# A mixture of experts on one core: a third shared tile in front of the expert blocks, table groups and gathers at other units

## The reference

```
x = x + self_attention(layernorm(x))            # 16 heads, one shared key/value head, causal
x = x + cross_attention(layernorm(x), ctx, pos) # 32 heads, axial rotary positions
h = layernorm(x)                                # 2048 tokens
probs = softmax(h @ router_w.T)                 # 16 experts
top 4 of 16, weights divided by their sum
routed = sum over the 4: (silu(h @ w_gate[e]) * (h @ w_up[e])) @ w_down[e] * weight     # 176 wide
shared = (silu(h @ sh_gate) * (h @ sh_up)) @ sh_down                                    # 704 wide
x = x + routed + sigmoid(h @ sh_gate_w) * shared
```

## Time and profile before

| what | us |
|---|---|
| median of three runs | 776.66 |
| profiled execution: its own time | 777.8 |
| its span | 776.0 |
| TensorE (PE) busy | 687.4 (89%) |
| VectorE (DVE) busy | 401.1 (52%) |
| POOL busy | 359.9 (46%) |
| ScalarE (ACT) busy | 301.4 (39%) |

### The profile page before, as it was taken

The page is one execution under the profiler, slowest core; times in us unless marked ns, Lnnn a source line. Parts: engine busy times, 40 slices in busy tenths (PEclk is TensorE's granted clock), DMA queues, the critical chain, the costliest instruction groups (busy, mean ns, idle before and its releaser), DMA issues. The chain is left out here.

```text
span 776.0 us, 18811 instructions
## 1 busy us (share of the span) xinstructions
PE 687.4 (89%) x6959; PEld 528.3 (68%) x6959; DVE 401.1 (52%) x917; ACT 301.4 (39%) x676; POOL 359.9 (46%) x451
## 2 busy tenths in 40 slices
PE   4799999876999999999757979299999999999975
PEld 4677777444887887877633868267777777777864
DVE  3546554326366666665257599542222222221998
ACT  1455655321244445444517423023333333333422
POOL 2357653332122212210027435547777777775634
PEclk9889999887599999999858989779999999999989
DMA  7000000012112111111046930113333333333931
GB/s 200 13 13 9 11 13 9 13 18 35 19 20 37 27 34 29 30 34 18 3 157 188 238 87 1 41 55 103 103 102 103 103 107 102 106 102 114 349 102 34
DMA packets 49558, 55.88 MB, mean 72 GB/s; under 512 B 8462, under 2 KB 43776, under 8 KB 49472
## 3 DMA queue, kind: packets, MB, share of 16 engines
q1 hardware_dynamic: 39124, 33.16, 16.1%
q0 software_dynamic: 7584, 20.72, 8.3%
q10 hardware_dynamic: 2764, 0.80, 0.5%
HBM read 34.34 MB, written 14.55 MB: 63 GB/s over the span
## 5 line engine op out<-in xcount | busy, mean ns | idle before, releaser
L1563 PE MATMUL s<-wx,routed_out 128*128 x316 | 109.1, 468 | 1.0 <-ACT routed_out L1266 1.0
L1434 DVE TENSOR_TENSOR routed_out<-s,routed_out 128x176 f32<-128x176 f32 x79 | 27.0, 342 | 141.9 <-ACT routed_out L1271 141.9
L1198 POOL DMA_INDIRECT slot_rows<-stage,dest x79 | 78.0, 987 | 35.5 <-issue 19.5
L735 ACT ACTIVATE b_pt<-s 128x1024 f32<-128x1024 f32 x64 | 63.5, 1020 | 79.0 <-PE s L787 79.0
L1164 POOL DMA_INDIRECT routed_in<-normed_rows,token x79 | 77.7, 983 | 31.0 <-issue 20.3
L1582 PE MATMUL last<-wx,routed_out 88*128 x316 | 81.5, 380 | 0.7 <-DVE routed_out L1439 0.7
L717 DVE TENSOR_REDUCE b_mx<-s 128x8 f32<-128x1024 f32 x32 | 39.2, 1225 | 75.9 <-PE s L832 75.9
L1563 PEld LDWEIGHTS s<-wx,routed_out 128*128 128x128 f32 x316 | 54.9, 194 | 18.8 <-issue 2.4
L1172 POOL TENSOR_TENSOR h_full<-h_full,silu_gate 128x512 f32<-128x512 f32 (+1 forms) x24 | 31.8, 1326 | 57.0 <-ACT h_full L1242 57.0
L1447 DVE SCALAR_TENSOR_TENSOR x_sb<-wx,share,x_sb 128x256 f32<-128x256 f32 x64 | 51.7, 825 | 11.9 <-DMA wx<-slot_rows 10.1
L1582 PEld LDWEIGHTS last<-wx,routed_out 88*128 88x128 f32 x316 | 53.7, 190 | 5.7 <-issue 1.5
(11 more groups left out here) (265 smaller groups left out, 1568.9 us busy)
## 6 DMA issues: line engine op xcount, KB each, us to landing
wx<-slot_rows SPq DMA_DIRECT2D x16, 512.0 KB, 8.8
b_qk<-b_rot SPq DMA_DIRECT2D x128, 32.0 KB
wx<-in_w_gate SPq DMA_DIRECT2D x4, 528.0 KB
wx<-in_w_up SPq DMA_DIRECT2D x4, 528.0 KB
wx<-in_w_down SPq DMA_DIRECT2D x4, 528.0 KB
x_sb<-in_x SPq DMA_DIRECT2D x4, 512.0 KB, 6.2
normed_rows<-stage SPq DMA_DIRECT2D x4, 512.0 KB, 3.9
out<-x_sb SPq DMA_DIRECT2D x16, 128.0 KB, 1.8
```

What stands on the lines that cost most here:

```text
L735: nc.scalar.activation(pt[:, c % 2, u].rearrange("p h q -> p (h q)"), s2[:, u].rearrange("p a n -> p (a n)"), ACT.Exp, scale=HD_B ** -0.5) ...
L1198: nc.gpsimd.indirect_dma_start(out=slot_rows[:, :], out_offset=bass.IndirectOffsetOnAxis(ap=dest[:, n:n + 1].bitcast(U32), axis=0), in_=ys ...
L1563: last = nc.tensor.matmul(s2[:, n % 2, 0, 0:2 * FE], xT[:, n % 2, P * k:P * k + P], wx[:, bass.ds(e, 1), 2 * FE * k:2 * FE * k + 2 * FE].r ...
```

## The change

ET becomes 3: eighteen units stand in front of the blocks, six behind. Table groups 0 to 7 move to units 8, 9, 10 (two), 11 (two), 12 and 13. The six gathers stand in pairs between `product` and `low_part` of units 15, 16 and 17. DVE's shared output of tile 0 stands behind group 1, that of tile 1 directly behind the token, ahead of the expert numbers, that of tile 2 behind the weights' arithmetic, ahead of the blocks, and that of tile 3 before b = 12. SP's outputs all wait for the DVE's last addition to their sequence. TensorE's code is the same but for the place of the groups; the bounds of the loops follow EARLY, now 18.

```diff
-ET = 2
+ET = 3
-RANK_AT, TABLE_AT, OUT_AT = 3, 6, 3
+RANK_AT, OUT_AT = 3, 1
+TABLE_AT = {8: (0,), 9: (1,), 10: (2, 3), 11: (4, 5), 12: (6,), 13: (7,)}
+GATHER_AT = {15: (0, 1), 16: (2, 3), 17: (4, 5)}
 # SP
-            for n in range(NB - 4):
+            for n in range(NB):
                 sp.wait_ge(x_final, n + 1)
-                sp.dma_start(out[n], x[:, n, :]).then_inc(stored, 16)
-            for n in range(NB - 4, NB):
-                if n < NB - 1:
-                    sp.wait_ge(x_final, n + 1)
-                else:
-                    sp.wait_ge(acc_out, NT)
                 sp.dma_start(out[n], x[:, n, :]).then_inc(stored, 16)
 # POOL, in the loop over the early units
                 if u < EARLY:
                     product(u)
-                else:
-                    pool.wait_ge(index_ready, 1)
-                    for a in range(2):
-                        pool.wait_ge(xn_stored[a], 16 * NR // 2)
-                    for n in range(AHEAD_G):
-                        if n % 4 == 0:
-                            pool.wait_ge(up_done, NCH * (n // 4 + 1))
-                        gather(n)
+                for n in GATHER_AT.get(u, ()):
+                    if n == 0:
+                        pool.wait_ge(index_ready, 1)
+                        for a in range(2):
+                            pool.wait_ge(xn_stored[a], 16 * NR // 2)
+                    if n % 4 == 0:
+                        pool.wait_ge(up_done, NCH * (n // 4 + 1))
+                    gather(n)
                 if u >= 1:
                     low_part(u - 1)
 # DVE
             nc.vector.tensor_scalar(token[:], dest[:], TOK - 1, None, ALU.bitwise_and).then_inc(index_ready, 1)
+            shared_out(1)
             ... (expert numbers)
-            shared_out(1)
             ... (weights)
+            shared_out(2)
             ... (blocks)
                 if b == BT * ET:
-                    shared_out(ET)
+                    shared_out(NT - 1)
                 ...
-                last.then_inc(y_used if b >= BT * (NT - 1) else x_final, 1)
-            dve.wait_ge(y_used, BT)
-            shared_out(NT - 1)
+                last.then_inc(x_final, 1)
 # TensorE, in the loop over the early units
-                if TABLE_AT <= u < TABLE_AT + TOPK * NB // HC:
-                    table_part(u - TABLE_AT)
+                for grp in TABLE_AT.get(u, ()):
+                    table_part(grp)
```

More of the change, by code:

```diff
@@ L1076, in mixture @@
     y_in = [sem(f"y_in{i}") for i in range(NB)]
-    y_used, x_final = sem("y_used"), sem("x_final")
+    x_final = sem("x_final")
     def rows_of(u):
@@ L1388, in shared_out @@
                                                           ALU.mult, ALU.add)
-                    if t == NT - 1 and i < BT - 1:
-                        last.then_inc(x_final, 1)
                 last.then_inc(acc_out, 1)
```

## The result

Over 20 runs of each, the median went from 776.64 to 782.73 us, 6.1 us or 0.8% more. The ratio, which goes by the fast runs of both kernels, is 1.0112, with a 95% interval of 1.0082 to 1.0143. The change made the kernel slower by about 1%; the interval is 6.4 to 11.1 us. The profiled execution of the kernel after took 782.33 us, its span 780.6.

What follows compares the result with a forecast made beforehand. It took routing on DVE and POOL's gathers to hold up the front, TensorE to bound the blocks and DVE the tail. Front +21.3 and tail -14.4 made span 782.9; the difference of 6.9 on the median gave 783.5, range 770.5 to 789.

Steps and rivals of the forecast that it cites:

- the walk: Front: step-by-step schedule of TensorE, DVE and POOL from unit 6, blocks starting at 529.2 instead of 506.42, +22.8 us.
- The price of a unit to DVE (2.2 us): Front: a one-hot group takes DVE 5.16 us beside a unit on POOL, 2.94 alone.
- A shared output isn't stretched: Front: DVE's shared output, reading PSUM, takes 1.65 us beside POOL, not 3.85; otherwise the sum is 4.4 us later.
- The order decides which wait remains: Front: down 12 needs the second shared output, over at 500.8, so TensorE waits 1.1 us there.
- The gathers: Front's end: gathers between product and low part make POOL's rounds 5.85 us, where TensorE needs 4.2; TensorE waits 4.3.
- The tail (-14.4): Tail, DVE bound: with six units instead of twelve, 45 multiply-adds run at 0.494 us; bounds -12.5 to -16.
- the blocks (-1.5): Start of the blocks: full clock instead of half for the first four blocks and first transposes, -1.5 us.
- +6.9: Whole span: front +21.3 and tail -14.4, 782.9 against 776.0.
- DVE keeps up: Rival, front: second shared output ready when TensorE reaches down 12, blocks at 517.7, total 772.0; chance 0.22.
- The clock holds: Rival, front: the same schedule without half-clock stretches, blocks at 524.2, total 778.3; chance 0.18.

Runs made afterwards that it cites:

- e3_pool_short: Kernel after, with POOL's product and low part on 128 of 512 columns from unit 2 on; 768.7 us.
- e5_spread: Kernel after, with one table group per unit, second shared output behind group 6, gathers behind low parts (one, one, four); ratio to before 0.9944, 768.5 us.
- e1_tail_six: Kernel before, without units 18 to 23 (shared expert of the fourth tile left out); 763.6 us.
- e2_gathers_behind: Kernel after, with all six gathers behind the last low part; 780.2 us, 1.0105 of before.
- e4_low_first: Kernel before, with the last early low part ahead of the six gathers instead of behind them; ratio to before 0.9905, 765.1 us.
- e6_third_tile_alone: Kernel after, with groups at units 6 to 13, shared outputs behind group 3 and the expert numbers, six gathers ahead of the last low part; 786.3 us.
- e7_spread_pairs_ahead: As e5_spread, but gathers in pairs ahead of the low parts of units 15, 16 and 17; 776.9 us.

## Why the prediction was right

It gave 783.5 us with 770.5 to 789; measured 782.73. More than the total, the steps can be held against the rows, since the walk was written out. Times of the kernel after are moved here by +3.98 us, to the time scale of the walk.

| step | walk | after, moved |
|---|---|---|
| group 1 done | 462.4 | 462.5 |
| first shared output over | 464.1 | 464.1 |
| TensorE's wait for it | 1.9 | 1.42 |
| groups 2, 3, 4, 5 done | 467.9, 473.0, 478.1, 483.2 | 468.3, 473.4, 478.5, 483.7 |
| wait for group 5 | 4.1 | 4.27 |
| unit 12 over | 490.1 | 491.2 |
| table read | 495.7 | 496.9 |
| token | 499.1 | 500.0 |
| second shared output over | 500.8 | 501.6 |
| wait for it | 1.1 | 0.38 |
| unit 15's hidden product over | 505.1 | 506.1 |
| wait for low part of unit 14 | 2.85 (worked out from the walk) | 1.78 |
| wait for low part of unit 16 | 4.3 | 4.29 |
| from unit 15 to the first transposes | 24.1 | 22.5 |
| first transposes | 529.2 | 528.6 |

That the last row fits to 0.6 us is in part luck: two misses cancel. TensorE came to the end of unit 15 1.0 us late: group 5 was 0.5 late, and the half clock behind it lasted 6 us (479.74 to 485.6) and not 5. And the way from there was 1.6 shorter: the first gather took 1.24 us and not 2.18, and of the two last down products only the first ran at the half clock.

*The price of a unit to DVE (2.2 us)* held: groups stayed at 5.1 us, and e3_pool_short shows that POOL's operations are the cause. *A shared output isn't stretched:* the open choice between 1.65 and 3.85 is decided by the rows of after. The output at 458.43 took 1.65 us while POOL's product ran from 458.93 on. That agrees with the rule cited for it from the Trainium skill's page "SBUF — State Buffer", section "Who interferes with whom". *The order decides which wait remains:* predicted for down 12 as 1.1, measured 0.38, since TensorE itself came 1.7 us later than in the walk (501.4 for 499.7) and the output 0.8. e5_spread shows the rest: take both away by order and the front loses 14.0 us together with the gathers' delay. *The gathers:* the walk's rounds of 5.85 us were 5.7 and 6.0; two kernels without pairs ahead of low parts were 6.1 and 6.7 us shorter in front than those with them. The first of the two low-part waits was 1.78 and not 2.85 because the first gather took 1.24 us. *The tail (-14.4):* -13.9, and -12.0 in e1_tail_six, which is -13.7 with the shared output of 1.65 that the change also takes out of the tail.

*Where it was off: the blocks (-1.5).* The prediction had the pipeline start at the full clock. The first transposes did (0.66 for four), but TensorE then waited 1.25 us, and the first gate and up products ran at the half clock again, 2.69 us as the 2.71 of the earlier trace rows. The blocks took 202.1, and between 200.5 and 202.2 in the others. This term was mis-sized by 1.8 us, which is nearly all of the difference between +6.9 and +8.6. The cold start is only the smaller part of that miss: from the first transposes to the fifth block's gate and up products it was 12.2 us (524.60 to 536.76) against 13.1 before (506.42 to 519.56), so 1.0 of the 1.5 was there. It was lost again further on: eighteen blocks between 603.80 and 650.05 us took 2.49 to 2.67 us each instead of 2.49, 1.4 us more in all, at the full clock; the kernel before has no such stretch. Its cause stays open.

*The rivals.* "DVE keeps up" had its point at down 12 by 496.4 on the walk's clock; it ran at 501.75. "The clock holds" fell too: after the 4.27 us wait the matmuls took 0.41 instead of 0.28. The half clock also came with the waits of 4.26, 4.01 and 4.01 us in e2_gathers_behind, e4_low_first and e6_third_tile_alone (first group products 1.24, 1.24 and 1.23 us where a warm one takes 0.73). Behind the wait of 3.73 us in e6_third_tile_alone the first matmul still ran at the full clock (0.35), and 0.45 us after the restart, at 501.19, the half clock came all the same. Before the wait of 3.79 us in e7_spread_pairs_ahead it was there already, from 509.16 on. So no wait of about 4 us kept the clock in any run. That a free-running window sets the moment, as the Trainium skill's page "TensorE: Matmul & The Clock Gate", section "What's actually happening", has it, would fit a fall that comes with the wait in one place and 0.45 us behind it in another; the runs don't show it.

So where did the expected gain go? The third tile is worth 13.9 us in the tail. In front it was to fill 16.4 us of idle. But more than half of the large hole was no hole: 7.3 us of it were a low part queued behind gathers of which the blocks needed only the first (e4_low_first). And the six units are work for TensorE too: 6 x 4.20 = 25.2 us, free only as far as they fill its idle time. Two short waits of the kernel before belong to that time:

```profile
487.66 0.39 PE L1508 MATMUL s<-sd,h_hi 128*128 128x256 f32 x1 [0.68 <-POOL h_lo L1160]
490.48 0.73 PE L1529 MATMUL last<-stage 128*128 128x158 bf16 x8 [1.13 <-DVE stage L1403]
```

Between unit 6 and the blocks TensorE's waits that have a row add up as follows:

| kernel | waits in front | rest of the front |
|---|---|---|
| before | 4.02 + 0.68 + 1.13 + 12.34 = 18.2 | 37.9 |
| after | 1.42 + 4.27 + 0.38 + 1.78 + 4.29 = 12.1 | 66.0 |
| e4_low_first | 4.01 + 0.74 + 2.22 + 4.63 = 11.6 | 37.1 |
| e5_spread | 1.41 + 1.98 + 0.76 = 4.2 | 60.0 |

The change filled 6.0 of the 18.2 us, and the rest of the front grew by 28.2 and not 25.2, in part because more of it ran at the half clock. With 13.9 us in the tail, some 11.3 (25.2 less 13.9) had to be filled to break even; that is an estimate at the full clock. e5_spread filled 14.0 and was faster than before. But once the low part has moved, only 11.6 us of idle are left, about what breaks even, and so e5_spread isn't ahead of e4_low_first.

The token came 6.6 us later after unit 6 than before (496.06 - 446.42 = 49.6 against 493.46 - 450.40 = 43.1), but not because POOL's added units slowed the groups: all eight were there at 39.1 us, 0.9 earlier than before. 4.7 of the 6.6 us are the table, read later because group 7's products on TensorE now stand behind the hidden products of units 12 and 13 as well; 1.9 are the five operations from the table to the token, which now lay beside a unit on POOL. Nor did the blocks wait for the token itself: the first gather came 8.4 us behind it, at 504.43, in its place in POOL's list, and in e5_spread the token came still later, at 51.5, with a front 14.0 us shorter. A unit does cost DVE as much in front (2.2 us) as in the tail (2.0, the 12.0 of e1_tail_six over six). In the tail that is the price, since DVE bounds it; in front most of the price is TensorE's own.

## What to carry to other kernels

Before an idle stretch is filled, ask why it is one: if the work that ends it only stands behind other work in an engine's list, reordering that list gets the time without anything to fill it. When work is moved into a stage, price it for each engine there: for the one with idle time it is free only as far as it fills that time (here 25.2 us of TensorE's work for 18.2 of idle, 7.3 of which were to be had otherwise), and it can delay another through a third (here POOL's elementwise operations DVE's). Work put between two links of a chain that turns once per unit costs its length in every round; behind the link that closes the round it fits into what is free.

## What the runs showed that was not expected

The clock falls without a long wait. In the kernel after it dropped at about 509.5, in the middle of a down product that itself had waited only 1.78 us, after a stretch with waits of 0.4 and 1.8 us between units; matmuls went from 0.28 to 0.41 us and came back at about 512.9. In e7_spread_pairs_ahead it dropped at 509.16, in the down product behind a wait of 1.95 us. In e5_spread waits of 1.98 and 0.76 us left it full. The drop cost the kernel after little: ACT's copy for unit 17 waited for TensorE until 514.33 instead of for the low part that ended at 513.94, some 0.3 us of POOL's round.

The hold between POOL and DVE works both ways. POOL's product at 498.09 in the kernel after took 2.19 us instead of 1.29 (e2_gathers_behind has the same at 495.17); it began while DVE's tensor_tensor of 497.66, 1.46 us long with two inputs in SBUF, ran.

The first gather took 2.18 or 2.19 us of POOL in the three kernels in which POOL had been idle for 6 us (before, e1_tail_six, e4_low_first), and 1.24 to 1.37 in the others, in which it followed a product or low part at once. The cause of the difference was not tried.
